# Second attention of a four-layer kernel: where VectorE makes its masks and compares ranks between the searches, and which heads' masks ScalarE makes

## The reference

```python
qkv = x @ W_qkv.T + b_qkv                       # 4 x 1024 tokens, 16 heads of 8
scores = einsum('bhid,bhjd->bhij', q, k) * scale
topk_scores, indices = lax.top_k(scores, 307)   # int(1024 * 0.3), for each row
masked = full_like(scores, -inf).at[..., indices].set(topk_scores)
attn = softmax(masked, axis=-1)
out = einsum('bhij,bhjd->bhid', attn, v) @ W_out.T + b_out
```

## Time and profile before

| | us |
|---|---|
| median of 3 runs (lowest, highest) | 3462.47 (3461.37, 3471.24) |
| the profiled execution's own time | 3468.05 |
| its span in the profile | 3466.3 |
| busy in the span: PE, DVE, ACT, POOL | 2636.8, 2752.5, 2452.2, 2014.0 |

### The profile page before, as it was taken

The page is one execution under the profiler, slowest core; times in us unless marked ns, Lnnn a source line. Parts: engine busy times, 40 slices in busy tenths (PEclk is TensorE's granted clock), DMA queues, the critical chain, the costliest instruction groups (busy, mean ns, idle before and its releaser), DMA issues. The chain is left out here.

```text
span 3466.3 us, 74747 instructions
## 1 busy us (share of the span) xinstructions
PE 2636.8 (76%) x23705; PEld 1489.1 (43%) x23705; DVE 2752.5 (79%) x8588; ACT 2452.2 (71%) x4051; POOL 2014.0 (58%) x4543
## 2 busy tenths in 40 slices
PE   3699999677645777777777777776777777758999
PEld 2233333233423454444455444443444444544444
DVE  5788888326439999999999999998999999844444
ACT  2266666433128999999999999997999999822221
POOL 3134333410228888888888888886888888640000
PEclk8699999888656777777777777776777777768999
DMA  5211221010230101101100110110110110010000
GB/s 149 89 52 49 53 56 30 12 34 16 75 56 2 15 5 17 18 2 17 17 9 11 17 16 4 17 17 2 17 18 2 17 17 2 2 32 3 7 7 9
DMA packets 115266, 85.88 MB, mean 25 GB/s; under 512 B 58154, under 2 KB 97340, under 8 KB 114876
## 3 DMA queue, kind: packets, MB, share of 16 engines
q1 hardware_dynamic: 106331, 75.20, 10.1%
q0 software_dynamic: 8192, 4.79, 0.9%
q10 hardware_dynamic: 352, 1.18, 0.1%
HBM read 54.25 MB, written 19.40 MB: 21 GB/s over the span
## 5 line engine op out<-in xcount | busy, mean ns | idle before, releaser
L1285 POOL TENSOR_TENSOR a_near<-a_side,a_z 128x1024 int32<-128x1024 int32 x512 | 969.0, 1892 | 42.6
L1181 PE MATMUL a_ST<-a_qs,a_ks 75*128 75x128 bf16 x4096 | 696.7, 259 | 336.0 <-ACT a_eT L1220 205.5
L1381 DVE MAX8 a_cand<-a_near 128x8 f32<-128x256 f32 x2048 | 750.8, 410 | 0.0
L1417 DVE TENSOR_SCALAR_CACHE_REDUCE a_z<-a_S,a_thr 128x1024 f32<-128x1024 f32 x512 | 649.1, 1268 | 81.2 <-issue 54.2
L1181 PEld LDWEIGHTS a_ST<-a_qs,a_ks 75*128 75x128 bf16 x4096 | 479.0, 118 | 526.1 <-issue 519.9
L1205 ACT ACTIVATE a_signs<-a_z,a_tiny 128x1024 bf16<-128x1024 f32 x512 | 589.3, 1151 | 76.7 <-DVE a_z L1417 70.3
L1198 ACT ACTIVATE a_signs<-a_S,search 128x1024 bf16<-128x1024 f32 x512 | 572.2, 1118 | 24.1 <-PE a_S L1134 24.0
L1220 ACT ACTIVATE a_eT<-a_ST 128x1024 f32<-128x1024 f32 x512 | 521.0, 1018 | 32.0 <-PE a_ST L1182 31.2
L776 ACT ACTIVATE a_eT<-a_ST 128x512 f32<-128x512 f32 (+3 forms) x768 | 329.3, 489 | 210.0 <-PE a_ST L761 148.9
L1134 PE MATMUL a_S<-a_ks,a_qs 72*128 72x512 bf16 x1024 | 409.1, 490 | 80.6 <-DVE a_z L1417 55.7
L880 DVE TENSOR_REDUCE a_mx<-a_S 128x1 f32<-128x512 f32 (+3 forms) x768 | 381.7, 548 | 77.9 <-PE a_S L748 68.2
(11 more groups left out here) (342 smaller groups left out, 4636.5 us busy)
## 6 DMA issues: line engine op xcount, KB each, us to landing
a_qs<-q_parts SPq DMA_DIRECT2D x174, 64.0 KB
a_ks<-k_parts SPq DMA_DIRECT2D x174, 64.0 KB
a_qs<-a_flip SPq DMA_DIRECT2D x512, 0.8 KB
q_parts<-p_qp SPq DMA_DIRECT2D x48, 128.0 KB, 1.8
k_parts<-p_kp SPq DMA_DIRECT2D x48, 128.0 KB, 1.8
a_qs<-q_parts SPq DMA_DIRECT2D x60, 96.0 KB
a_ks<-k_parts SPq DMA_DIRECT2D x60, 96.0 KB
f_w<-L_ffn_W SPq DMA_DIRECT2D x16, 256.0 KB, 2.9
```

Of the source, the lines that this page charges most:

```text
L1181: pe.matmul(ST[:, block_of], ks[:, base(hl) + kb * P:base(hl) + (kb + 1) * P], qs[:, tile(hl):tile(hl) + P], start=True, stop=False)
L1285: pool.tensor_tensor(near[:, hl % NEARS, :].bitcast(I32), side[:, one].bitcast(I32).broadcast_to([P, SEQ]), z[:, hl % H, :].bitcast(I32), ...
L1381: mm = dve.max(found[:, 8 * g:8 * g + 8], near[:, h2 % NEARS, g * SW:(g + 1) * SW])
L1417: dve.tensor_scalar(z[:, h1 % H, :], S[h1 % 2][:, :], thr1[:, h1 % H:h1 % H + 1], None, ALU.add, ALU.max, accum_out=zmax[:, h1 % H:h1 % H ...
```

## The change

1. Masks: unit l has its mask made by ACT if l % 8 is 1, 5 or 7, otherwise by DVE (`by_act`; `acted` counts ACT's masks for the waits). Before, ACT made those of all odd l. Per eight units DVE makes 5 masks and ACT 3, instead of 4 and 4.
2. In DVE's slots the mask stands between the third and the fourth search, behind the list (`away_made`), in odd slots and in those with h % 8 == 2. In slots with h % 4 == 0 the comparison's steps stand between and behind the searches.
3. In slots with h % 8 == 6 DVE reads the flags' counts before it divides, PE's sums of flags no longer wait for `normed`, and a copy of one number into `idle` is gone.

```diff
+        by_act = lambda l: l % 2 == 1 and l % 8 != 3
+        acted = lambda l: sum(by_act(x) for x in range(l + 1))
...
-                    shown = quad(it, h, NL) + 2
-                    pe.wait_ge(normed, min(max(shown, 1), QUADS + 1) if isinstance(it, int) else shown)
                     pe.matmul(FL, k.ones[:, 0:1], signals[:, h0:h0 + 8, :].rearrange("p j c -> p (j c)"), start=True, stop=True).then_inc(flag_p, 1)
...
-                    pe.wait_ge(mask_a if hl % 2 else mask_s, it * (UN // 2) + (h - TURN) // 2 + 1)
+                    pe.wait_ge(*((mask_a, acted(l)) if by_act(l) else (mask_s, l + 1 - acted(l))))
...
-                                       minus_b[:, :] if hl % 2 else k.ident_b[:, :], start=False, stop=True)
+                                       minus_b[:, :] if by_act(l) else k.ident_b[:, :], start=False, stop=True)
...
-                if lagged(it, h, PICK, UN, TOTAL) is not None and (h - PICK) % 2:
+                if lagged(it, h, PICK, UN, TOTAL) is not None and by_act(nth(it, h, PICK)):
...
+                def away_made():
+                    if lagged(it, h, PICK, UN, TOTAL) is not None and not by_act(lp):
+                        dve.wait_ge(cut_s, it * QU + (h - PICK) // 4 + 1)
+                        if lp >= MASKS:
+                            dve.wait_ge(turned, lp - (MASKS - 1))
+                        dve.tensor_scalar(mask[:, hp % MASKS, :], z[:, hp % H, :], cut[:, hp % H:hp % H + 1], AWAY,
+                                          ALU.is_lt, ALU.mult).then_inc(mask_s, 1)
...
-                    if h1 % 2 and not (isinstance(it, int) and l1 < H):
-                        dve.wait_ge(mask_a, it * (UN // 2) + (h - C2) // 2 - (H // 2 - 1))
+                    if l1 >= H and by_act(l1 - H):
+                        dve.wait_ge(mask_a, acted(l1 - H))
...
                     near_made()
+                    top(0)
+                    rest_made()
+                    sort_last()
+                    top(1)
                     if has4 is not None:
...
                                           wide(rank[:, four], WINDOW), ALU.is_equal).then_inc(choice_s, 1)
-                    rest_made()
-                    sort_last()
+                    top(2)
...
                         dve.tensor_tensor(picked[:, :, :], hits[:, :, :], best[:, ring4, :], ALU.mult).then_inc(choice_s, 1)
-                    top(0)
+                    top(3)
...
                         dve.tensor_reduce(edge[:, four], picked[:, :, :], AX, ALU.add).then_inc(edge_s, 1)
-                    top(1)
...
-                    top(2)
-                    top(3)
                 elif h % 2:
...
-                    if lagged(it, h, PICK, UN, TOTAL) is not None:
...
+                    top(0)
                     rest_made()
                     sort_last()
-                    for g in range(SEGS):
-                        top(g)
+                    top(1)
+                    top(2)
+                    away_made()
+                    top(3)
                 else:
+                    if closes(it, h):
+                        group = groups(it, h)
+                        dve.wait_ge(flag_p, group + 1)
+                        dve.tensor_scalar(seen[:, :], FL, 1.0, None, ALU.mult, ALU.add, accum_out=flag_sum[:, :]).then_inc(flag_v, 1)
...
                     top(1)
                     top(2)
-                    if closes(it, h):
-                        group = groups(it, h)
-                        dve.wait_ge(flag_p, group + 1)
-                        dve.tensor_scalar(seen[:, :], FL, 1.0, None, ALU.mult, ALU.add, accum_out=flag_sum[:, :]).then_inc(flag_v, 1)
+                    away_made()
                     top(3)
                     if closes(it, h):
...
-                        dve.tensor_copy(idle[:, 2 * (h % H) + 1:2 * (h % H) + 2], half[0:1, :])
```

More of the change, by code:

```diff
@@ L1438, in slot @@
                         dve.tensor_reduce(edge[:, four], picked[:, :, :], AX, ALU.add).then_inc(edge_s, 1)
-                    top(1)
-                    if has4 is not None:
                         open_ends = cand[:, ring4, :].rearrange("p j (g r) -> p j g r", r=8)[:, :, :, 7]
@@ L1457, in slot @@
                     near_made()
-                    if lagged(it, h, PICK, UN, TOTAL) is not None:
-                        dve.wait_ge(cut_s, it * QU + (h - PICK) // 4 + 1)
-                        if not (isinstance(it, int) and lp < MASKS):
-                            dve.wait_ge(turned, lp - (MASKS - 1))
-                        dve.tensor_scalar(mask[:, hp % MASKS, :], z[:, hp % H, :], cut[:, hp % H:hp % H + 1], AWAY,
-                                          ALU.is_lt, ALU.mult).then_inc(mask_s, 1)
+                    top(0)
                     rest_made()
                     sort_last()
-                    for g in range(SEGS):
-                        top(g)
-                else:
+                    top(1)
+                    top(2)
+                    away_made()
+                    top(3)
+                else:
+                    if closes(it, h):
+                        group = groups(it, h)
+                        dve.wait_ge(flag_p, group + 1)
+                        dve.tensor_scalar(seen[:, :], FL, 1.0, None, ALU.mult, ALU.add, accum_out=flag_sum[:, :]).then_inc(flag_v, 1)
                     q, hn = quad(it, h, NL), here(h, NL + 3) % H
```

## The result

The changed kernel takes 3385.05 us (3382.78 to 3388.7, 4 runs) against 3464.64 for the kernel before on the same chip: 0.9769, with a 95% interval of 0.9751 to 0.9787. The profiled execution took 3384.95 us, its span is 3383.2.

The account below looks back on a forecast made before the run. DVE's slots were taken to bound the kernel. Per group of eight, -1.46 + 0.68 + 0.16 - 0.06 + 0.13 = -0.55 us, times 62 is -34 us: 3428 us forecast, range 3403 to 3478.

Parts of the forecast that it names:

- Reading the flags earlier is the same instruction in another place, 0: DVE's read of the flags' counts, slots h % 8 == 6: moving it earlier changes nothing, 0 us.
- nothing comes back at all: Rival for DVE's group of eight slots: collision savings kept without new losses, -0.90 us, -56 in all, 3406 us; chance 0.15.
- Masks and `hits`: DVE's collisions with POOL's `near`: the new places save 0.82 us on four masks and 0.64 on two `hits` per group.
- One more mask: DVE makes a fifth mask per group of eight slots: +0.68 us.
- `edge` and `signals`: DVE's comparison: `signals` right behind `edge` needs its result, leaving 0.08 us open twice per group, +0.16.
- Short collisions: DVE's masks or `hits` meeting POOL's short instructions in place of `near`: +0.13 us per group, 1.33 at most.
- rival C: No change: short collisions on DVE at their upper end, 0.7 us per group in place of 0.13, 3462 us; chance 0.10.
- I count 0: PE's sums of flags: their 2.1 us wait for `ctx` goes, but DVE's idle 0.92 and ACT's mask hide its worth, 0.
- the counts are there: DVE's read about 1.3 us into the slot: PE reached its sums before the slot began, so no wait.
- The 30.3 us: ACT's need for a group of eight slots with four masks, a floor below which DVE could gain nothing.
- Rival D: Slower: POOL's `thr` queues behind the moved mask and delays `z`, up to +0.70 us per group, 3506 us; chance 0.13.
- Rival E: Far slower: DVE's `signals` wait 1.68 us for POOL's `near` twice per group, +174 us, 3637 us; chance 0.02.

Follow-up runs that it names:

- Part 3 alone: Kernel before with only the flags' counts read at the slot's start and PE's sums not waiting for `normed`, copy into `idle` kept: 3449.45 us.
- parts 1 and 2: Changed kernel with the late read of the flags and PE's wait for `normed` put back, no copy into `idle`: 3453.44 us.
- sums first: Changed kernel with PE's sums of flags ahead of its product with v in slots h % 8 == 6: 3403.11 us.
- sums last: Changed kernel with PE's sums of flags placed behind `ST` in their slot: 3456.43 us.
- part 2 alone: Kernel before with only the new places of masks and comparison; ACT makes all odd masks, late read and copy kept: 3417.77 us.
- four of eight: Changed kernel with ACT making the masks of all odd units again, new places and early read kept: 3384.36 us.

## Why the prediction was wrong

The sign, the bound (DVE's slots) and the collisions were right. The size was not, and one step carries most of that.

**The step that failed: "Reading the flags earlier is the same instruction in another place, 0".** The instruction costs the same, but the register load and branch wait for its result. I had read their price myself, 0.92 us in a group, and treated it as fixed to the load's place. (Even that was misread: 32.8 us in 42 groups is 0.78, since every other group has 0.63.) It is a latency that begins with the read: from the read's start to the next `z` 1.34 or 1.63 us in the trace of before. Moved from 2.76 to about 1.6 into the slot, it is covered. Part 3 alone brings slot 6 from 4.25 to 3.38; in the change it goes to 3.64, as the counts come late in more than half of the groups. Forecast for slot 6: the copy's 0.06. Measured: 0.61. The 0.55 between them, times 62, is 34 of the 46 us that were missing. In the rivals the same mistake stands: even "nothing comes back at all" keeps the load, so the range's low end was no bound.

**Masks and `hits`.** Forecast 0.82 and 0.64; measured 4 x (0.956 - 0.735) = 0.88 and 2 x (0.530 - 0.207) = 0.65. Right. The way to the new place was partly wrong: I put `near` at 3.07 to 3.4 into a slot, behind the mask. It starts between the last 0.44 us of a slot and 0.91 into the next, and lets go before the mask.

**One more mask.** Forecast +0.68; measured 2041.32 - 2040.67 = 0.65 to the next start.

**`edge` and `signals`.** Forecast +0.16. `signals` starts 0.23 behind `edge`, 0.10 more than the 0.13 that an instruction of this size takes to the next, so +0.20. **Short collisions**: forecast +0.13; masks of 735 ns leave none, 0, and rival C with them. The sum is -0.88 + 0.65 - 0.65 + 0.20 = -0.68 of the 0.73 measured for the seven kinds of slots; `picked`, 240 ns before and 206 now, twice in a group, is another 0.07.

**PE's sums.** "I count 0" and "the counts are there" were both off. The counts are late in 25 of 42 groups, up to 0.6 us; they are in time with four masks on ACT, which the forecast did not connect with them. And taking PE's wait for `ctx` out of `ST`'s way is what keeps part of the gain of parts 1 and 2 from being lost in the chain by `ST`, exponential, count 1 and `thr`. That the place of the sums makes and unmakes this chain is shown by the runs with sums first and with sums last. It takes the fifth mask too: in part 2 alone, PE's wait in place, ACT's exponential waits 5.6 us for `ST` and POOL's `scaled` 9.3. The forecast let DVE's idle 0.92 and ACT's mask hide that wait and looked no further along the chain. Of the 1.09 us in a group that part 3 adds to parts 1 and 2 (30.65 - 29.56), 0.61 lie in slot 6, the load less the wait for the counts, and 0.48 in the others, the chain. A late read without PE's wait was not tried, since nothing would then order the two accesses to the PSUM tile.

**ACT.** The 30.3 us was the group less ACT's idle time, so each instruction counted to its end. A queued one starts before that: in the run with four of eight ACT's durations add up to 1671 us from 1100 to 2350, a stretch of 1250. So the same four masks fit into a group of 29.56, where ACT is busy without a pause. That ScalarE makes fewer masks changes nothing measurable beside the other two parts.

**Rival D** (`thr` late) is 0.2 us in the change and real where ACT or PE lag: 6.1, 8.0 and 19.8 us in the runs above, never more than 0.2 at a time. **Rival E** (`signals` behind `near`) did not occur: the two `signals` last 182 and 221 ns on average. The order that the Trainium skill gives (SBUF — State Buffer, Who interferes with whom), that whoever issues first goes through, agrees with the run of part 3 alone, where `near` began first more often and the mask took 1048 ns on average.

## What to carry to other kernels

A value that an engine loads into a register or branches on should be produced as early as the queue allows: in this kernel the latency counted from its producer, not from the load's place in the code, and it was free with 2.05 us of queued work between, not quite with 1.54. Before costing a move at nothing, list what consumes its result. Where two engines shut each other out, a saving in one slot shifts them against each other, so a part tried alone tells little about its worth in the whole, and every slot has to be looked at, not only the one that was edited.

## What the runs showed of the hardware

The register load and branch had two lengths in the kernel before, `z` 1.34 or 1.63 us behind the read in alternate groups; why they alternate was not looked into. Idle time put down to issue vanished altogether with 2 us of work queued between read and `z` (0.0 in part 3 alone, and in the change with sums last), and 0.11 of it was back in every other group with 1.54 queued. And an engine's pause has a worth: removing 0.87 us of it from slot 6 cost 0.55 in collisions elsewhere in the group, when the masks stood in their old place.
